# Output of a gated-attention block: one store of a row group, or four stores of a chunk each a step later

## The reference, cut to what matters

```
y   = x + tanh(g_xattn) * Wo(window_attention(Wq(layernorm(x)), Wk(ctx), Wv(ctx)))   # 8 heads, window of 16 positions
out = y + tanh(g_ffn)  * (flat * w_sum + w_dense @ expert_bias)
      # flat = layernorm(y), over the 2048 positions of a channel;
      # w_dense: the top 8 of softmax(flat @ router_weight.T + router_bias), 64 experts
```

## Time and profile before

| | |
|---|---|
| Time, median of three runs | 1553.32 us |
| The profiled execution: its own time | 1557.26 us |
| The profiled execution: span from first to last instruction | 1555.1 us |
| Mean granted TensorE clock, as a share of full speed | 0.972 |
| Busy: TensorE matmul, VectorE, ScalarE, GpSimd | 94%, 82%, 74%, 74% of the span |
| Read from HBM, written to it | 136.88 MB, 33.55 MB |
| Stores of the output | 32 of 1024 KB, 7.0 us from issue to landing (median) |

### The profile page before, as it was taken

How to read it: one execution, slowest core, us unless ns; L and a number is a source line. 1 busy time by engine, 2 the same in 40 slices (tenths; PEclk the granted TensorE clock), 3 DMA queues, 4 the chain that set the end, 5 groups by cost and what they waited for, 6 DMA issues and landing times.

```text
span 1555.1 us, 66658 instructions
## 1 busy us (share of the span) xinstructions
PE 1464.6 (94%) x28162; PEld 1199.9 (77%) x28162; DVE 1276.5 (82%) x2970; ACT 1144.8 (74%) x2009; POOL 1148.0 (74%) x1110
## 2 busy tenths in 40 slices
PE   4799999999999999999999999999999999999985
PEld 3687887888787888878788788878888887778764
DVE  5578987888898887988888898888889888788764
ACT  4687877777787877788787877778787787767652
POOL 4688777787777877877787887778778777677661
PEclk8899999999999999999999999999999999899896
DMA  7455455445546554454555545455554545434132
GB/s 230 125 140 126 106 173 131 123 149 143 147 121 172 141 131 146 121 157 128 149 149 141 156 119 159 128 146 147 144 159 114 159 132 142 121 98 128 44 81 85
DMA packets 365577, 210.39 MB, mean 135 GB/s; under 512 B 294497, under 2 KB 295521, under 8 KB 361057
## 3 DMA queue, kind: packets, MB, share of 16 engines
q1 hardware_dynamic: 365280, 206.14, 49.1%
HBM read 136.88 MB, written 33.55 MB: 110 GB/s over the span
## 4 chain that ended last, share of the span: by engine, by line
PE 46%; DVE 35%; issue 8%; POOL 5%; ACT 3%; DMA 2%; SPq 1%; POOLq 0%; DVEq 0%; ACTq 0%
PE ps_j L1117 18%; PE ps_s L1177 7%; PE ps_a L1142 6%; PE ps_r L1219 5%; DVE prob_t L900 5%; PE ps_s L1117 3%; DVE p_sum L890 3%; DVE st_x L907 2%; DVE wq_lo L822 2%; POOL prob L493 2%; DVE lg L1046 2%; DVE st_in L804 2%; DVE v_turn L871 2%; PE ps_s L1172 2%; PE ps_a L1196 2%
## 5 line engine op out<-in xcount | busy, mean ns | idle before, releaser
L486 POOL TENSOR_TENSOR score<-score,p_inv 128x384 f32<-128x384 f32 x256 | 221.6, 866 | 119.5 <-DVE p_inv L894 117.0
L493 POOL TENSOR_TENSOR prob<-score,prob 128x384 f16<-128x384 f32 x256 | 266.0, 1039 | 38.8 <-ACT prob L644 38.3
L1177 PEld LDWEIGHTS ps_s<-kv_win,q_col 32*32 32x32 f32 x16384 | 198.0, 107 | 57.8 <-issue 57.8
L1177 PE MATMUL ps_s<-kv_win,q_col 32*32 32x48 f32 x16384 | 234.1, 205 | 2.4 <-issue 2.2
L900 DVE STREAM_TRANSPOSE prob_t<-prob 128x512 f32<-128x512 f32 x256 | 176.7, 699 | 55.1 <-POOL prob L493 54.9
L467 POOL TENSOR_TENSOR c_lo<-c_in,c_hi 128x1024 fp32r<-128x1024 f32 x64 | 152.7, 2386 | 89.5 <-ACT c_hi L618 89.5
L1142 PEld LDWEIGHTS ps_a<-prob_t,v_diag 128*128 128x128 f16 x6528 | 175.3, 98 | 50.1 <-DVE prob_t L900 32.6
L1142 PE MATMUL ps_a<-prob_t,v_diag 128*128 128x48 f16 (+2 forms) x6528 | 187.6, 183 | 26.2 <-DVE prob_t L900 19.4
L462 POOL TENSOR_TENSOR att_lo<-att,att_hi 128x512 fp32r<-128x512 f32 x128 | 161.8, 1275 | 51.5 <-ACT att_hi L604 50.3
L1117 PE MATMUL ps_j<-c_hi,wkv_hi 128*128 128x512 f32 x512 | 171.3, 416 | 19.6 <-DVE kv_win L864 10.6
L890 DVE TENSOR_REDUCE p_sum<-score 128x8 f32<-128x384 f32 x256 | 139.2, 544 | 54.3 <-ACT score L638 53.6
(11 more groups left out here) (149 smaller groups left out, 3318.0 us busy)
## 6 DMA issues: line engine op xcount, KB each, us to landing
v_diag<-v_turn SPq DMA_DIRECT2D x512, 68.0 KB, 2.8
c_in<-ctx_dram SPq DMA_DIRECT2D x64, 512.0 KB, 4.9
x_in<-x_dram SPq DMA_DIRECT2D x64, 512.0 KB, 5.5
x_res<-x_dram SPq DMA_DIRECT2D x64, 512.0 KB, 4.3
out_dram<-x SPq DMA_DIRECT2D x32, 1024.0 KB, 7.0
c_sq<-ctx_dram SPq DMA_DIRECT2D x60, 512.0 KB, 5.5
x<-ctx_dram SPq DMA_DIRECT2D x4, 512.0 KB, 6.1
x<-experts_dram SPq DMA_DIRECT2D x2, 512.0 KB, 10.6
```

The lines of the kernel that those rows point to most:

```text
L486: pool.tensor_tensor(score[:, u], score[:, u], p_inv[:, u, :].unsqueeze(2).to_broadcast([P, HALF, KEYS]), ALU.mult).then_inc(pm_rdy, 1)
L493: pool.tensor_tensor(part(prob[:, u % 2], 1)[:, :, 0:KEYS], score[:, u], part(prob[:, u % 2], 0)[:, :, 0:KEYS], ALU.subtract).then_inc(pl_ ...
L1177: ins = pe.matmul(s[head(h), n * KEYS:(n + 1) * KEYS], q_col[head(h), g, at:at + SUB], kv_win[c % 2][head(h), 0, g, at:at + KEYS], start=F ...
```

## The change

SP no longer stores a row group in the step that finishes it. It stores it in the next step, behind that step's `x_in` load, as four DMAs of one chunk each: 128 rows of 2 KB, 256 KB. So row group 0 goes out in step c = 3 (not c = 2), row group 1 in step c = 0 of the next sequence (not c = 3). In the last step of the program SP stores the four chunks of the last row group as well, each behind a wait for its own finish. The counts that ScalarE and SP wait for are changed to match: each row group now raises `out_st[g]` by 64. All else is as before.

```diff
+        def finished(b, c):
+            at, db = (c - 1) % NCH, (c - 1) // NCH
+            return finishing(b + db, at)
...
+            def store(g, b, j):
+                need(sp, fin_rdy, final(b, g, j))
+                sp.dma_start(out[b, g * P:(g + 1) * P, cols(j)], x1[b % 2][:, g, cols(j)]).then_inc(out_st[g], 16)
...
-                if finishing(b, c):
-                    g = c - 2
-                    rows_out = out[b - 1, g * P:(g + 1) * P, :]
-                    need(sp, fin_rdy, final(b - 1, g, NCH - 1))
-                    sp.dma_start(rows_out, x1[1 - par][:, g, :]).then_inc(out_st[g], 16)
+                if finished(b, c):
+                    for j in range(NCH):
+                        store((c - 1) % NCH - 2, (b if c else b - 1) - 1, j)
+                if b == B and c == 3:
+                    for j in range(NCH):
+                        store(G - 1, B - 1, j)
...
-                sp.wait_ge(out_st[g], 16 * (B + 1))
+                sp.wait_ge(out_st[g], 16 * NCH * B + 16)
...
-                        need(act, out_st[g], b * 16)
+                        need(act, out_st[g], (b - 1) * 16 * NCH + 16)
```

## The result

The change made the kernel slower. In twelve runs of each, side by side on one chip, its median was 1565.95 us (1558.12 to 1574.5) against 1554.74 us (1550.95 to 1559.56): a ratio of 1.007, with a 95% interval of 1.0047 to 1.0093. The forecast was 1551.6 us.

A forecast was written before the change was run, and what follows sets the result against it. TensorE was taken to bound the kernel, sharing c = 3 with VectorE, and DMA bandwidth no step. Five terms of 0 and -1.7 us at the end took the plain-run median of 1553.32 to 1551.6 us, range 1548.6 to 1556.2.

The forecast's parts named there:

- SP's wait for the last finish: On SP's queue, in the run's body: removing the wait before the store was to give 0 us.
- More issues on SP: On SP: 128 stores in place of 32, four issues taking 1.9 us before the next v_diag block; cost 0 us.
- x_in: Load in c = 3 and c = 0: store behind it adds at most 0.4 us, within slack; 0 us; late-load rival 4%.
- The `v_diag` copies and ScalarE's wait: Copies behind the stores keep over 10 us of slack, ScalarE's buffer wait stays already met; 0 us each.
- The end: After the last finish: only a quarter of the last store waits, landing sooner; gain of 1.7 us, between 1.1 and 1.9.
- the v_diag floor of 2.2: At the end: 68 KB v_diag copies never landed in under 2.2 us, so the last piece was taken to need that.
- The transfers move: DMA traffic: c = 3 hardly changes, c = 2 loses a megabyte, c = 0 gains one; no load late, 0 us.
- the first rival: TensorE's instruction waits move from the start of c = 3 to that of c = 1; slower, 1559.5 us; chance 8%.

## Why the prediction was wrong

The prediction, 1551.6 us in 1548.6 to 1556.2, gave "slower" 0.13. The measured median lies above the range, at 1565.95 us, or 11.2 above the one of before in its own comparison.

- **SP's wait for the last finish: 0 us, as predicted.** The wait went (of SP's remaining 30.3 us, 27.6 are the eight waits at the end, and thirteen of 0.2 us stand in c = 3) and gave nothing. The `v_diag` block starts where it did.
- **More issues on SP: 0 us, as predicted.** Four issues took 2.48 us (from 709.57), not 1.9, and ended long before the next block at 719.61. Pieces at the old place measured 1.0011.
- **x_in: 0 us, as predicted.** It landed in 5.8 to 5.9 us in c = 3 (once 6.2), where 5.5 to 5.9 was forecast; one landed at 418.3, and its reader came at 418.56: slack of 0.3 us. VectorE never waited for it in the body; the run with the pieces ahead of `x_res` shows what would follow if it did. In c = 0 the store behind it added 0.8 us (5.1 to 5.9), not at most 0.4, well within the slack there.
- **The `v_diag` copies and ScalarE's wait: 0 us, as predicted.** Neither has a wait in the trace after.
- **The end: -1.7 us forecast, -1.6 measured** (4.4 to 2.8 us). The last piece landed in 2.0 us, under the v_diag floor of 2.2 that I took, 1.8 less than the megabyte; but from the landing to the end of the span it was 0.75 us, for 0.46 before. The two runs with the end alone, 0.9986 and 0.9979, are 2.2 to 3.3 us by their ratios, with intervals that hold 1.7.
- **The failed step is "The transfers move", in its part on c = 0.** It asked what the new megabyte there could make late and went through data only: x_in, and in the terms after it `v_diag` and ScalarE's buffer. It set 0 us. But TensorE's code comes through the same DMA engines, and the term measured 11.8, 7.9 and 9.4 us over before's 0.2 in three profiles (8 to 12 us). In c = 3 the table falls by 2.7 to 3.2 us, most of which may be the stretch at the lower clock in before's one profile.

The mechanism stood in the text as the first rival, down to its place (start of c = 1, behind the store of c = 0, waits over 0.6 us) and to its cost being free in c = 3. What was wrong is its chance, 8%, and its price. The price forecast was 5 us of waits and one stretch at the lower clock for 2.9. Measured were four waits of 0.96 us, 3.8 us in sum, and a stretch of 3.4 to 6.8 us at a granted clock of 0.50 behind each, so that a wait cost 1.9 to 3.6 us. The rival's 1559.5 is 6.2 us above the kernel before; the three comparisons have 11.2, 6.6 and 11.4 us. As a reason against it I gave that the store in c = 3 has no such wait behind it. The shift by 128 instructions shows what that was worth: the same store then has ten of them. It was not that the store there is harmless; at the starts of c = 0 the blocks happened not to fall due behind it. I had the earlier trace rows, five waits just as a store ends, and read the empty place as evidence of absence.

The place was not even empty. I had looked at the starts of steps alone. The trace of the kernel before has a sixth wait on issue over 0.6 us, 5.7 us into a step c = 0 behind the store that SP issued in c = 3 at 224.48. It is longer than the five, and the step took 25.62 us for 22.2, with the lower clock for a part of it: most of the 2.7 us that before has in c = 0 in the table. TensorE's timeline of before, and busy times by stretch:

```profile
237.51 0.73 PE L1117 MATMUL ps_j<-att_hi,wo_hi 128*128 128x512 f32 x2 [1.84 <-issue]
...
231.78:257.40 25.62, 23.39 (x443) 19.06 (x443) 17.62 (x45) 18.19 (x31) 18.76 (x19) 0.93 0.41 107
```

It stands at the same remainder, 194 of 256. The kernels that are not shifted and have a store at that place in c = 3 have the wait too, 1.6 to 1.9 us long, in all profiles but one; the kernel without a store in c = 3 (only row group 1 late) and the one whose store goes out sooner (ahead of `x_res`) do not have it. So the trace that I read spoke against the reason that held the rival at 8%: behind a store in c = 3 TensorE did wait for code in c = 0, and the step was 3.4 us longer.

The Trainium skill, "Runtime: NRT & Kernel Launch", section "Instruction fetch mechanics", says that each engine's instructions come in blocks of 16 KiB, 256 instructions, by a DMA queue of its own, and calls the cost of crossing a block "mostly hidden". This case agrees on the size: 3.65 MB in 223 packets, all waits at one remainder by 256, and a shift by 256 instructions leaves the waits at their instructions while one by 128 moves them. On "hidden" the measurement decides: waits of up to 2.3 us stood open behind a megabyte of stores.

## What to carry to other kernels

Here bulk stores stood in the way of the code of an engine that runs a long unrolled stream, so before a store is moved in such a kernel, look at the queue of instruction packets and at waits on "issue" in the trace: in which step do they fall, and does the engine that fetches bound that step. Look through the whole step, not at its start alone. A place behind which another engine sets the pace is the one for bulk traffic; a place that looks free may only lie well to the code's blocks, and a shift by half a block shows which it is. When such a kernel is tuned by a few tenths of a per cent, any edit that adds instructions to the fetching engine is a test of alignment too: here 128 of them were worth -0.7% to +2%, more than the edit under study.

The version with the lowest ratio keeps row group 0 in c = 2, moves row group 1 to c = 0, stores both in pieces, and shifts the code by 128 instructions: 0.9977 and 0.9984, the second with an interval that touches 1. The kernel before with only its end in pieces does as well within the intervals (0.9986, 0.9979) with a smaller edit. Both hold for one place of the code only: unshifted the first is 1.0044, and shifted the second is 1.0077.

## What the runs showed of the hardware that I had not expected

- **A code block waits for a backlog of data.** The block's packet moved 3.1 us later in its step with a megabyte ahead of it (19.8 us in, not 16.7), and with two, another came 26.2 us after the start of c = 3 in place of 24.0. The Trainium skill, "DMA: Bandwidth & Descriptors", section "Queues, rings and completion order", has an engine take turns among its queues, packet by packet. By that rule a block would wait for a packet or so; this trace shows it behind the megabyte. Why, the runs don't tell.
- **Code is not used at once when its packet ends.** The 109 waits end 1.2 to 1.7 us after it (1.25 us for the one of 719.48).
- **A wait of about 1 us can be followed by 3.4 to 6.8 us at 1.2 GHz,** in which TensorE is busy throughout. It came behind all four waits at c = 1 in the change's profile, behind none of the same waits in the one with the code shifted by 256, and within 4 us behind 40 of the 109 in all. What decides it stays open. The spread of the runs goes with the clock: the change's run with a mean clock of 0.978 took 1558.1 us, the one with 0.967 took 1574.5. In which steps those runs lost it, no trace shows.
- **256 KB land in 2.0 us** at the end of the run, with nothing beside them, where 1 MB took 3.9.
- **Not explained:** that the end alone with the shift measured 1.0077 where the change with the same shift measured 1.016, though their waits look alike in the one profile of each.
